# Taking the pauses out from in front of the row gathers on GpSimd in a two-layer LSTM graph kernel

## The reference

```python
def _lstm_last(seq, wih, whh, bih, bhh):        # seq: 33 steps x 512 nodes x 128
    def step(carry, x_t):
        h, c = carry
        g = x_t @ wih.T + h @ whh.T + b
        i, f, gg, o = jnp.split(g, 4, axis=-1)
        c = sigmoid(f) * c + sigmoid(i) * tanh(gg)
        h = sigmoid(o) * tanh(c)
        return ((h, c), None)
...
def _sage_conv(x, src, ...):
    msgs = x[src].reshape(n, d, c)              # d = 33
    aggr = _lstm_last(jnp.swapaxes(msgs, 0, 1), wih, whh, bih, bhh)
    return aggr @ wl.T + bl + x @ wr.T
...
h = relu(_sage_conv(x, src, ...conv1)); y = _sage_conv(h, src, ...conv2)
x = layernorm(x + y)
hr = einsum('ni,rio->rno', x, weight); msg = hr[rel_type, src] * norm[:, None]
x = layernorm(x + relu(segment_sum(msg, dst, 512)))
```

## Time and profile before

| | us |
|---|---|
| three runs | 528.24, 525.88, 529.69 (median 528.24) |
| profiled execution, by the same clock as the runs | 524.9 |
| its span, first to last instruction | 523.1 |
| TensorE busy | 481.5 (92%) |
| VectorE busy | 415.0 (79%) |
| ScalarE busy | 334.4 (64%) |
| POOL busy | 351.6 (67%) |
| mean granted TensorE clock | 0.979 |

### The profile page before, as it was taken

One profiled execution on the slowest core, in us unless ns is written; L12 is line 12 of the kernel. 1 busy time (PEld: TensorE's weight loads), 2 busy tenths in 40 slices (PEclk: granted clock), 3 DMA queues, 4 the chain that ended last, 5 costly groups with the idle time before them and its releaser, 6 DMA issues.

```text
span 523.1 us, 10333 instructions
## 1 busy us (share of the span) xinstructions
PE 481.5 (92%) x3599; PEld 361.0 (69%) x3599; DVE 415.0 (79%) x1134; ACT 334.4 (64%) x851; POOL 351.6 (67%) x485
## 2 busy tenths in 40 slices
PE   8499999999999979899999999999999987979785
PEld 3378887888888865688888888889855443434343
DVE  3569989989999975888888888889879866565655
ACT  1466877677767754677676777677657554555452
POOL 6658877887787832788888878877046556555660
PEclk9799999999999999999999999999999998979899
DMA  4855565555655632555556555655021111111110
GB/s 159 335 161 163 163 179 155 158 168 167 174 155 162 179 97 100 162 142 162 161 158 167 162 143 164 163 161 159 22 86 36 45 37 40 41 40 37 41 40 26
DMA packets 25907, 66.32 MB, mean 127 GB/s; under 512 B 6278, under 2 KB 10174, under 8 KB 25728
## 3 DMA queue, kind: packets, MB, share of 16 engines
q0 software_dynamic: 18048, 55.85, 37.8%
q1 hardware_dynamic: 6720, 8.89, 5.4%
q10 hardware_dynamic: 1088, 0.92, 0.6%
HBM read 62.48 MB, written 3.16 MB: 125 GB/s over the span
## 4 chain that ended last, share of the span: by engine, by line
PE 50%; DVE 18%; DMA 15%; ACT 8%; issue 6%; POOL 2%; DVEq 0%; ACTq 0%; POOLq 0%
PE gates L1240 20%; DMA edge_rows<-msg_table,msg_index 12%; PE gates L1233 7%; PE gates L1185 5%; PE work L1240 5%; PE work L1162 5%; DVE prod_fc L901 3%; DMA code<-in_x,src_steps 3%; DVE h_full L872 3%; DVE prod_ig L903 3%; DVE msg_full L1087 2%; ACT act_if L606 2%; ACT h_hi L596 2%; ACT msg_full L743 2%; PE work L1233 2%
## 5 line engine op out<-in xcount | busy, mean ns | idle before, releaser
L524 POOL DMA_INDIRECT rows<-gate_table,src_steps x192 | 198.6, 1034 | 53.8 <-POOL pause L522 51.3
L537 POOL DMA_INDIRECT edge_rows<-msg_table,msg_index x76 | 76.8, 1011 | 67.6 <-ACT msg_full L743 25.9
L1240 PE MATMUL gates<-h_hi,whh_hi 128*128 128x256 f16 x396 | 100.7, 273 | 4.2 <-ACT h_hi L596 2.6
L1240 PE MATMUL gates<-h_hi,whh_lo 128*128 128x256 f16 x396 | 100.4, 273 | 0.0
L600 ACT ACTIVATE act_if<-gates 128x512 f32<-128x512 f32 x96 | 57.4, 598 | 50.5 <-PE gates L1240 50.4
L522 POOL MEMSET pause<- 128x256 f32 x199 | 66.9, 336 | 33.6 <-DMA gate_table<-rows 17.3
L1240 PE MATMUL gates<-h_lo,whh_hi 128*128 128x256 f16 x396 | 85.5, 274 | 0.4 <-DVE h_lo L885 0.4
L1233 PE MATMUL gates<-ident,rows 128*128 128x128 f32 x584 | 79.7, 273 | 3.6 <-issue 3.4
L1233 PEld LDWEIGHTS gates<-ident,rows 128*128 128x128 f32 x584 | 67.0, 141 | 7.5 <-issue 4.6
L901 DVE TENSOR_TENSOR prod_fc<-act_if,cell 128x256 f32<-128x256 f32 x128 | 53.8, 421 | 20.4 <-ACT act_if L600 9.6
L1077 DVE TENSOR_SCALAR rows<-node_iota,dst_f 128x512 f16<-128x512 f16 x132 | 43.2, 361 | 28.4 <-ACT msg_full L743 28.3
(11 more groups left out here) (180 smaller groups left out, 1000.4 us busy)
## 6 DMA issues: line engine op xcount, KB each, us to landing
rows<-gate_table,src_steps POOLq DMA_INDIRECT x192, 3.5
gate_table<-rows SPq DMA_DIRECT2D x8, 256.0 KB, 2.0
src_direct<-direct_rows SPq DMA_DIRECT2D x1, 2048.0 KB, 7.7
edge_rows<-msg_table,msg_index POOLq DMA_INDIRECT x76, 2.5
code<-code_table SPq DMA_DIRECT2D x6, 160.0 KB, 3.8
msg_table<-table_sb SPq DMA_DIRECT2D x4, 192.0 KB, 1.9
code<-code_table SPq DMA_DIRECT2D x5, 128.0 KB, 3.5
whhT<-turned_whh SPq DMA_DIRECT2D x2, 256.0 KB, 7.7
```

What stands on the lines that cost most here:

```text
L524: pool.indirect_dma_start(target, None, table, bass.IndirectOffsetOnAxis(src_steps[:, t, k:k + 1], axis=0)).then_inc(landing(l, t, k)[0], 16)
L537: pool.indirect_dma_start(edge_rows[:, c % 2, n, :], None, msg_rows, bass.IndirectOffsetOnAxis(msg_index[:, pool_first(c) + n:pool_first(c ...
L1240: mm = pe.matmul(gate_place(t, h, gate), w[:, gate * P:(gate + 1) * P], state[:, h, :], start=(opens and opens_bank(t, gate) and n == 0), ...
```

## The change

The memset of `pause` and the wait for it are taken out from in front of every gather of the two layers. The steps' letters stay as they are, so one step in four in the first 27 of a layer is still a picked one.

```diff
--- before
+++ after
@@ -518,9 +518,6 @@
                         pool.wait_ge(*landing(*issued[at - UNDER_WAY]))
                     target, table = ((x_rows[:, x_slot(l, t, k), :], x) if by_x_row
                                      else (rows[:, row_slot(l, t, k), :], gate_table[l]))
-                    if at > 0:
-                        pool.memset(pause[:, :], 0.0).then_inc(paused, 1)
-                        pool.wait_ge(paused, at)
                     pool.indirect_dma_start(target, None, table, bass.IndirectOffsetOnAxis(src_steps[:, t, k:k + 1], axis=0)
                                             ).then_inc(landing(l, t, k)[0], 16)
```

## The result

The changed kernel is slower: 573.83 us median (571.81 to 582.45), against 527.48 for the kernel before on the same chip; ratio 1.087, 95% interval 1.082 to 1.092.

What follows compares the result with a forecast made beforehand. POOL's gather pitch was taken to set when rows arrive, mattering only where TensorE stands still for them. Gains of 2.9 + 0.6 + 0.5 = 4.0 us, taken off the 528.24 median, gave 524.2 us, range 520.5 to 529.0.

Steps and rivals of the forecast that it cites:

- The new pitch: POOL's gathers: 1.33 us apart instead of 1.63; POOL then waits for freed slots in layer 0's last third.
- The end of layer 0: Last steps of layer 0: TensorE's three waits for gathered rows go, gaining 2.9 us (bounds 2.4 and 3.4).
- The start: Gathers of x rows: the eighth starts earlier, xg_lo of step 1 moves from 22.18 to 21.23; 0.6 us gained.
- VectorE's builds: One-hot builds beside POOL's gathers: less stretched, gaining 0.5 us in layer 0 (bounds -2.9 and +1.5).
- fifth part: Layer 1's gathers, the edge stage and the memset's traffic: the change costs and gains nothing there.
- step 3: Start of the program: x rows gathered sooner, xg_lo of step 1 earlier; 0.6 us gained (bounds 0.47 and 0.95).
- steps 1 to 4: Gather pitch, end of layer 0 (2.9 us), start (0.6) and one-hot builds (0.5): together 4.0 us gained.
- C: Slower: close gathers hold VectorE's one-hot builds back; 541 us at half a gather each; chance 0.11.
- D: Slower through VectorE's some 630 recurrent operations: 14 ns each is 9 us; chance 0.04.
- B: Nothing gained: with three gathers in flight each lands later, needing 4.9 us instead of 3.5; 527.8 us; chance 0.13.
- A: More gain: all build stretch goes, start gives 0.95 us, layer 0's tail 3.4; 522.4 us; chance 0.14.

Runs made afterwards that it cites:

- x_no_pause: The kernel before without the pauses in front of the eight gathers of x rows only; the 192 others keep theirs: 530.49 us, ratio 1.005.
- plain_copies: The changed kernel with each of its 192 gathers from the gate table replaced by a plain copy of 128 neighbouring rows: 521.76 us, ratio 0.991.
- the short rows: Gathers of 512-byte rows: the kernel before with a one-column memset, 580.72 us, ratio 1.101; the changed kernel without pause, 579.78 us, ratio 1.102.
- half_rows: The changed kernel with 64 rows instead of 128 fetched by each gather from the gate table: 594.61 us, ratio 1.128.
- fours: The kernel before with three whole memsets in front of a time step's first gather and none before its other three: 533.27 us, ratio 1.015.

## Why the prediction was wrong

I forecast 524.2 us (520.5 to 529.0) and 0.62 for no change; it was 573.8.

1. **The new pitch** was right: median gap 0.30 us, pitch 1.31 (forecast 1.33), and POOL then waits for `gates`, 74.0 us, as the waits show. It does so from 64.7 us on and not only in the layer's last third, since the slots come free late. (From 15.46 to 187.18 are 96 intervals, 1.79 us each, not 97; nothing hangs on it.)

2. **The end of layer 0** was right in the kernel itself. POOL issues the layer's last gather at 194.3 in a layer that ends at 216.5, and the timeline of VectorE has the last steps at 4.64, 4.65 and 4.19 us (start of one second-half `h_full` to the next), where before the last two took 5.68 us and 5.83 (`h_full` at 190.49 and 196.32). Over the last four steps it is 18.5 us in place of 21.3, a gain of 2.8 where I had 2.9:

```profile
202.56 0.42 DVE L869 SCALAR_TENSOR_TENSOR h_full<-act_o,tanh_c 128x256 f32<-128x256 f32 x1
...
207.20 0.42 DVE L869 SCALAR_TENSOR_TENSOR h_full<-act_o,tanh_c 128x256 f32<-128x256 f32 x1
...
211.85 0.42 DVE L869 SCALAR_TENSOR_TENSOR h_full<-act_o,tanh_c 128x256 f32<-128x256 f32 x1
...
216.04 0.42 DVE L869 SCALAR_TENSOR_TENSOR h_full<-act_o,tanh_c 128x256 f32<-128x256 f32 x1 [0.48 <-ACT tanh_c L589]
```

3. **The start** came about as forecast (21.2): `xg_lo` at 20.85 in after, at 21.24 in x_no_pause. Its worth, 0.6 us, was wrong on its own, as x_no_pause shows; there a gain ahead of a stretch that POOL's pitch limits is taken back. In after itself the loss covers it, so there it can't be told.

4. **VectorE's builds** came out inside the 0.48 to 0.60 us that the prediction named: a mean of 501 ns between 40 and 170 us, where it was 563. `h_full` stayed at 419 ns. The group of the builds in after, 40 to 170 us:

```profile
L811 DVE TENSOR_SCALAR src_onehot<-src_direct,block_iota 128x512 f16<-128x512 int32 x20 | 9.6, 501 | 0.0
```

5. **The step that failed** is the sentence that a gather matters only where TensorE stands still for rows, with its fifth part, "Free: ... the memset's traffic hides nothing". The sum counted rows and VectorE's time, and put the price of close gathers for TensorE at nothing. What the runs showed in its place: with the pauses gone 156 of TensorE's messages come late, by up to 9.65 us, and the layers take 44.9 us longer. The pause kept POOL's gathers far enough apart for these messages to pass, and of this the trace of before shows nothing, since it has not one late message. plain_copies comes nearest to the sum without this effect: at a ratio of 0.991, it gains 4.9 us of its 527.0 us before, where I had 4.0. But plain copies are shorter than gathers (548 ns), and step 3's share was worth nothing by itself, so that the two figures lie close is in part luck; that steps 1 to 4 would be worth 4 us with gathers is not shown.

**The rivals.** C came closest: POOL's close gathers hold another engine up. It named VectorE, with 541 us at half a gather each; the one-hot builds became shorter instead. TensorE, the engine that was held, doesn't appear in it. The Trainium skill's page "SBUF — State Buffer", Who interferes with whom, gives as its single rule for overlapping work that "only the shared port pair causes contention", the pair of VectorE and GpSimd. The builds at 501 ns show no further cost from that pair with closer gathers. TensorE's late messages, up to 9.65 us, are a delay between overlapping engines that this rule, which speaks of the memory's ports, doesn't cover. D (the recurrent operations) is refuted by 419 ns. B (landings) is not what happened: it needed landings of 4.9 us, and the 28 of the 192 gathers of after whose landing is fully recorded took 3.7 us (median); and the short rows, at a quarter of the bytes, lost the same. A (more of the same gains) has about the time of plain_copies, 521.8 against 522.4, by luck: this is another kernel. The real rival was missing: a message between engines that is late, although each engine is on time.

What would have pointed to it: the kernel before has a 128x256 memset that writes nothing anyone reads, with a wait, in front of every gather, 0.60 us each. The prediction asked only what it costs and not what else could need the room.

## What to carry to other kernels

Where a profile shows an engine waiting for "remote" or "issue" while the engine it depends on has long ended, set the times of the semaphore changes against the ends of the instructions that make them. In this kernel, where TensorE's messages pace a recurrence, evenly spaced gathers on GpSimd at one in 1.55 us held nothing back; at 1.5 us (a spacer of 192 columns with a wait, gap 0.54 us) a few messages were late, up to 1.12 us, and the kernel was still 0.4 to 0.7% faster than with 256 columns; at 1.45 us one kernel lost nothing and one 4%; at 1.4 us and closer (on the mean of the closest four) all lost 9% and more. Shorter or fewer rows buy no closer gathers.

## What the runs showed of the hardware that I had not expected

- Close gathers on GpSimd hold back TensorE's semaphore changes by up to 9.65 us in after and 18.94 in half_rows, and never ScalarE's or VectorE's (at most 0.013 us, of those recorded, in all sixteen kernels).
- Fewer bytes (512 in place of 2,048 a row) or fewer rows (64 in place of 128 a gather) don't lessen the effect: 1.102 and 1.128 against 1.087. A gather takes 969 ns for 64 rows and 1012 for 128.
- A plain copy of 256 KB on the same queue takes POOL 0.54 us (median), and one in 0.94 us (over four) holds nothing back.
- Held changes keep their order, with no exception in any kernel. They come out singly while gathers go on (61.82, 63.26, 64.67 in after) and together once POOL pauses (77.21, 77.26 and 77.31 in fours, 1.13 to 0.57 us late).
